# A patch-token, attention and expert layer: inner chunks in twos, their 64-row products in pairs on the two halves of the rows

## What is computed

```
logits = flat @ Wr                       # 8 experts, two chosen for each token
order = argsort(-score)[:, :capacity]    # capacity 3920 tokens for each expert
dispatch = flat[order]
gate = silu(einsum('ech,ehi->eci', dispatch, w1))     # h = 192, i = INNER = 768
up = einsum('ech,ehi->eci', dispatch, w3)
expert_out = einsum('eci,eih->ech', gate * up, w2) * weight_sel[..., None]
routed = zeros.at[order].add(expert_out)
shared = silu(flat @ s1) * (flat @ s3) @ s2
out = h + routed + shared
```

## Time and profile before

| what | value |
|---|---|
| median of three runs | 3695.66 us (3693.1 to 3698.46) |
| the profiled execution | 3705.55 us, span 3703.7 us |
| PE busy | 3398.9 us, 92% |
| PE weight loads busy | 2416.6 us, 65% |
| DVE busy | 2472.7 us, 67% |
| ACT busy | 1570.9 us, 42% |
| POOL busy | 1432.8 us, 39% |
| granted TensorE clock, mean | 0.87 |

### The profile page before, as it was taken

The page is one execution under the profiler, slowest core; times in us unless marked ns, Lnnn a source line. Parts: engine busy times, 40 slices in busy tenths (PEclk is TensorE's granted clock), DMA queues, the critical chain, the costliest instruction groups (busy, mean ns, idle before and its releaser), DMA issues. The chain is left out here.

```text
span 3703.7 us, 76882 instructions
## 1 busy us (share of the span) xinstructions
PE 3398.9 (92%) x26932; PEld 2416.6 (65%) x26932; DVE 2472.7 (67%) x4826; ACT 1570.9 (42%) x3198; POOL 1432.8 (39%) x1302
## 2 busy tenths in 40 slices
PE   5999999999999999998249999899999999999997
PEld 4777777777777777776226566666666666666665
DVE  5988898888888989897645555554454444445443
ACT  2444444444444445443014444344444444444443
POOL 0222232222222222232215553136556555555664
PEclk8787788877877888775569999999999999999999
DMA  3332333223323332222012222213232232323222
GB/s 95 71 69 61 75 82 69 68 70 80 69 62 75 82 69 73 65 53 56 35 50 63 66 72 71 83 31 66 38 61 42 59 63 39 60 38 61 41 40 31
DMA packets 330541, 227.05 MB, mean 61 GB/s; under 512 B 209103, under 2 KB 309551, under 8 KB 326159
## 3 DMA queue, kind: packets, MB, share of 16 engines
q1 hardware_dynamic: 259536, 163.94, 17.4%
q0 software_dynamic: 57472, 48.46, 8.8%
q10 hardware_dynamic: 13262, 10.65, 0.8%
HBM read 107.75 MB, written 67.85 MB: 47 GB/s over the span
## 5 line engine op out<-in xcount | busy, mean ns | idle before, releaser
L1272 DVE SCALAR_TENSOR_TENSOR ffn_hidden<-ffn_up,ffn_silu 128x490 f32<-128x490 f32 (+2 forms) x534 | 358.1, 672 | 802.3 <-ACT ffn_silu L1255 731.4
L699 POOL TENSOR_TENSOR weights<-weights,x_pair 128x400 f32<-128x400 f32 x384 | 397.2, 1034 | 918.1 <-DVE weights L563 733.7
L1255 ACT ACTIVATE ffn_silu<-ffn_gate 128x490 f32<-128x490 f32 (+2 forms) x534 | 310.9, 583 | 702.4 <-PE ffn_up L1223 635.7
L615 DVE RECIPROCAL recip<-x_product 128x200 f32<-128x200 f32 x384 | 534.4, 1392 | 0.0
L1240 PE MATMUL ffn_out<-ffn_w_hi,ffn_hidden_hi 128*126 128x192 f16 (+2 forms) x2124 | 522.5, 246 | 0.0
L1242 PE MATMUL ffn_out<-ffn_w_hi,ffn_hidden_lo 128*126 128x192 f16 (+2 forms) x2124 | 522.4, 246 | 0.0
L1241 PE MATMUL ffn_out<-ffn_w_lo,ffn_hidden_hi 128*126 128x192 f16 (+2 forms) x2124 | 522.3, 246 | 0.0
L1428 POOL DMA_INDIRECT out_rows<-done,kept x256 | 425.9, 1664 | 150.4 <-issue 98.1
L1418 POOL DMA_INDIRECT tokens<-dram_x,ids x256 | 279.6, 1092 | 397.5 <-issue 258.9
L750 PE MATMUL bank<-w_qkv,normed_t 96*128 96x192 f32 (+1 forms) x1024 | 399.8, 555 | 19.1 <-ACT normed_t L413 19.1
L1265 DVE TENSOR_TENSOR ffn_hidden_lo<-ffn_hidden,ffn_hidden_hi 128x490 f16<-128x490 f32 (+2 forms) x534 | 355.4, 666 | 8.4
(11 more groups left out here) (181 smaller groups left out, 7429.8 us busy)
## 6 DMA issues: line engine op xcount, KB each, us to landing
patches<-in_patches SPq DMA_DIRECT2D x32, 1176.0 KB, 5.1
ffn_raw<-in_w SPq DMA_DIRECT2D x18, 768.0 KB
dram_x_t<-x_t SPq DMA_DIRECT2D x32, 392.0 KB, 3.1
x_t<-dram_x_t SPq DMA_DIRECT2D x24, 512.0 KB, 5.2
base<-dram_h SPq DMA_DIRECT2D x24, 384.0 KB
out_rows<-sums ACTq DMA_DIRECT2D x24, 384.0 KB
v_held<-v SPq DMA_DIRECT2D x64, 102.0 KB, 2.3
dram_h<-h SPq DMA_DIRECT2D x32, 192.0 KB
```

The costliest lines, as they stand in the source:

```text
L615: nc.vector.reciprocal(recip[:, n % 2], x_product[:, n % 2]).then_inc(inverted, 1)
L699: nc.gpsimd.tensor_tensor(weights[:, n % 4], weights[:, n % 4], x_pair[:, n % 4, ::-1], ALU.mult)\
L1255: nc.scalar.activation(T.silu[:, m % 2, 0:n], T.gate[m % 2][:, 0:n], ACT.Silu, scale=1.0 / (TOKEN_SCALE * WEIGHT_SCALE)).then_inc(T.silued, 1)
L1272: nc.vector.scalar_tensor_tensor(T.hidden[:, m % 2, 0:n], T.up[m % 2][:, 0:n], HIDDEN_SCALE / (TOKEN_SCALE * WEIGHT_SCALE), T.silu[:, m % ...
```

## The change

The chunks of a unit go two at a time, in three blocks. In a block, the four products of each chunk and output that use all 128 rows come first, 16 in all. Then come the four with `w_lo` and the far high tokens: those for gate use rows 0 to 63, those for up rows 64 to 127, with `far_again`, a second copy of the far high tokens, in these rows. Each is a product of 64 rows, and the two of a chunk stand on the two halves. `gated` now rises twice for each chunk.

`tensor_out` is cut into thirds of eight (tile, chunk) groups, and one stands behind each block. `turn` stands behind the first block, ahead of the first third. The token tiles have two slots, and the splits of the next unit are made after silu 3 (ScalarE) and `hidden` 3 with `hidden_lo` 2 (VectorE), instead of after the last chunk. ScalarE makes one more activation there, of 64 rows. `w_lo` is made in all 128 rows, and the memsets go.

```diff
-            for w_lo in T.w_lo:
-                for lo in w_lo[0:2]:
-                    n += 1
-                    nc.gpsimd.memset(lo[D - 128:128, INNER:2 * INNER], 0.0).then_inc(enlarged, 1)
-                    pool.wait_ge(enlarged, n)
...
+def tokens_hi(nc, T, slot, near, far, n):
+
+    nc.scalar.activation(T.near_hi[slot][:, 0:n], near, ACT.Copy, scale=TOKEN_SCALE).then_inc(T.tokens_hi, 1)
+
+    nc.scalar.activation(T.far_again[slot][D - 128:128, 0:n], far[D - 128:128], ACT.Copy, scale=TOKEN_SCALE)
+    nc.scalar.activation(T.far[slot][:, 0:n], far, ACT.Copy, scale=TOKEN_SCALE).then_inc(T.tokens_hi, 1)
...
+def tensor_pair(nc, pe, T, g, slot, ws, n, pair):
+
+
+    if pair == 0:
+        pe.wait_ge(T.tokens_lo, 2 * g + 6)
+    near_hi, near_lo, far, far_again = (x[slot][:, 0:n] for x in (T.near_hi, T.near_lo, T.far, T.far_again))
+    top, low = slice(0, D - 128), slice(D - 128, 128)
+    for m in (2 * pair, 2 * pair + 1):
 
         pe.wait_ge(T.multiplied, MI * g + m + 1)
         near = slice(m * 128, (m + 1) * 128)
-        far = slice(INNER + m * 128, INNER + (m + 1) * 128)
+        beyond = slice(INNER + m * 128, INNER + (m + 1) * 128)
...
             nc.tensor.matmul(out, hi[:, near], near_hi, start=True, stop=False)
             nc.tensor.matmul(out, hi[:, near], near_lo, start=False, stop=False)
             nc.tensor.matmul(out, lo[:, near], near_hi, start=False, stop=False)
-            nc.tensor.matmul(out, hi[:, far], far_both, start=False, stop=False)
-            last = nc.tensor.matmul(out, lo[:, far], far_both, start=False, stop=True)
-        last.then_inc(T.gated, 1)
...
+            nc.tensor.matmul(out, hi[:, beyond], far, start=False, stop=False)
+    for m in (2 * pair, 2 * pair + 1):
+        beyond = slice(INNER + m * 128, INNER + (m + 1) * 128)
+        nc.tensor.matmul(T.gate[m % 2][:, 0:n], T.w_lo[ws][0][top, beyond], far[top], start=False, stop=True)\
+          .then_inc(T.gated, 1)
+        nc.tensor.matmul(T.up[m % 2][:, 0:n], T.w_lo[ws][1][low, beyond], far_again[low], start=False, stop=True)\
+          .then_inc(T.gated, 1)
...
+    share = len(tiles) * MI // 3
+    for k in range(third * share, (third + 1) * share):
+        t, m = divmod(k, MI)
...
     for m in range(MI):
-        act.wait_ge(T.gated, MI * g + m + 1)
+        act.wait_ge(T.gated, 2 * (MI * g + m + 1))
...
         if m:
             hi(m - 1)
+        if m == 3:
+            split()
     hi(MI - 1)
...
-                tensor_unit(nc, pe, T, g, ws, XU)
-                if not closing(e, i, 7):
-                    turn(v + 1, half + i % 2, 1 - i % 2)
...
+                for part in range(3):
+                    tensor_pair(nc, pe, T, g, 1 - i % 2, ws, XU, part)
+                    if part == 0 and not closing(e, i, 7):
+                        turn(v + 1, half + i % 2, 1 - i % 2)
...
+                        tensor_out(nc, pe, T, g - 1, i % 2, 1 - ws if i == 0 else ws, ROUTED, part)
```

More of the change, by code:

```diff
@@ L1145, in sb @@
         return ctx.enter_context(nc.sbuf_tensor(f"ffn_{name}", shape, dt))
[L1147 to L1149 removed]
+    T.near_hi, T.near_lo, T.far, T.far_again = (
+        [sb(f"tokens_{name}{s}", [128, ST], F16) for s in range(2)] for name in ("near_hi", "near_lo", "far", "far_again"))
     T.silu = sb("silu", [128, 2, ST])
@@ L1174, in lower_parts @@
 def lower_parts(T, ws):
-    near, far = (slice(0, 128), slice(0, INNER)), (slice(0, D - 128), slice(INNER, 2 * INNER))
-    whole = (slice(0, 128), slice(0, MI * D))
+    near, far, whole = slice(0, INNER), slice(INNER, 2 * INNER), slice(0, MI * D)
     for n, parts in enumerate(((near, far), (near, far), (whole,))):
         for part in parts:
-            yield T.raw[n][part], T.w_hi[ws][n][part], T.w_lo[ws][n][part], part is parts[-1]
+            yield T.raw[n][:, part], T.w_hi[ws][n][:, part], T.w_lo[ws][n][:, part], part is parts[-1]
 def weights_lo(nc, T, ws):
@@ L1231, in tensor_out @@
+def tensor_out(nc, pe, T, g, slot, ws, tiles, third):
+    if third == 0:
+        pe.wait_ge(T.lo_ready, MI * g + MI + 2)
     w_hi, w_lo = (w[ws][2][:].rearrange("p (m n) -> p m n", m=MI) for w in (T.w_hi, T.w_lo))
     per = len(tiles) // 2
[L1233 to L1243, removed]
@@ L1246, in scalar_unit @@
-def scalar_unit(nc, act, T, g, slot, n):
+    share = len(tiles) * MI // 3
+    for k in range(third * share, (third + 1) * share):
+        t, m = divmod(k, MI)
+        n, c = divmod(t, per)
+        if m == 0 and c == 0:
+            pe.wait_ge(T.out_used, 2 * g + n + 1)
+        at, rows = tiles[t]
+        out = T.out[n][0:rows, c * D:(c + 1) * D]
+        hi, lo = T.hidden_hi[slot][:, m, at:at + rows], T.hidden_lo[slot][:, m, at:at + rows]
+        nc.tensor.matmul(out, hi, w_hi[:, m, :], start=(m == 0), stop=False)
+        nc.tensor.matmul(out, hi, w_lo[:, m, :], start=False, stop=False)
+        last = nc.tensor.matmul(out, lo, w_hi[:, m, :], start=False, stop=(m == MI - 1))
+        if m == MI - 1 and c == per - 1:
+            last.then_inc(T.out_full, 1)
@@ L1247, in hi, with scalar_unit @@
+def scalar_unit(nc, act, T, g, slot, n, split):
     def hi(m):
@@ L1478, in unit @@
             def unit(g, half, slot, tiles):
[L1479 to L1483, removed]
+                for part in range(3):
+                    tensor_pair(nc, pe, T, g, slot, 0, columns_of(tiles), part)
+                    if part == 0 and tiles is SHORT:
+                        turn(0, 0, 0)
+                    if not (isinstance(g, int) and g == 0):
+                        tensor_out(nc, pe, T, g - 1, 1 - slot, 0, WHOLE, part)
             shared_units(pe, unit)
@@ L1537, in unit, with split_next @@
             def unit(g, half, slot, tiles):
[L1538 to L1544, removed]
+                def split_next():
+                    if tiles is SHORT:
+                        split(0, 1)
+                    elif isinstance(g, int) and g == SHARED - 2:
+                        split_shared(half + 1, 0, TAIL)
+                    else:
+                        split_shared(half + slot, 1 - slot, ST)
+                scalar_unit(nc, act, T, g, slot, columns_of(tiles), split_next)
                 if not (isinstance(g, int) and g == 0):
```

71 lines of the change are left out of this document (33 added, 38 removed).

## The result

The changed kernel took 3710.8 us (median of 20 runs), the kernel before 3696.7 us in the same comparison: a ratio of 1.0036, 95% interval 1.0021 to 1.0051. The change makes the kernel 0.36% slower. The forecast was 3699 us, with a range of 3664 to 3735 that holds the result; "slower", the likeliest of the three signs by a little, came true. The profiled execution took 3710.33 us, its span 3708.5 us.

The account below looks back on a forecast made before the run. TensorE was taken to set the pace. Routed units -7, weights +21, shared units -14, seam +5 and tail -1 sum to +4 us on a profiled 3705.55 us; with the median 10 us lower, 3699 us, range 3664 to 3735.

Parts of the forecast that it names:

- slower: Sign of the forecast: the kernel's time rises by more than 0.2%; chance 0.39, against faster 0.34 and same 0.27.
- Products: TensorE's routed unit: halves save 1.24 us, mode switches cost 0.6, so 19.60 becomes 18.96 us.
- Case E: Rival: halves of the rows don't run together, routed unit 20.2 us, kernel 3774 us; chance 0.06.
- Order: Between blocks: a third of the output (1.97 us) covers the 1.6 us of clearing `gate` and `up`; no cost.
- The wait that takes the place: Routed units: earlier transposes wait for gathered rows, 19.48 us a unit, so 62 units gain 7 us, not 40.
- the cycle: Routed stage: transposes, rest of unit, `put`, scatter, landing, ids, gather, transposes; 38.96 us for two units.
- Case C: Rival: VectorE's bunched work collides with gathers and scatters, path 19.6 us, unit 19.98, kernel 3730 us; chance 0.22.
- Weights for the next expert: Seven expert starts: `hidden` 3.4 us late, scatter 3.8 late, 4.0 us together against 1.0 now; 21 us lost.
- Shared units: Shared stage: halves save 1.30 us less 0.6 of switching; 0.6 us a unit taken, 14 us gained.
- The seam: From shared to routed units: more work stands behind the first wait for rows; about 5 us lost.
- wrong altogether: What would refute the forecast: a clock that falls in the 4 us gaps of TensorE; no size given.
- Case A: The forecast itself: the rows cycle eats the gain, 3699 us, own range 3685 to 3713; chance 0.45.

Follow-up runs that it names:

- e1: The changed kernel with the remainder products as 128-row products again (halves undone), its order kept: 3731.7 us, ratio 1.0118.
- e5: The changed kernel with halves in the old order (blocks back to back, then transposes, then all output): 3891.5 us, ratio 1.057.
- e2: The changed kernel with the transposes of the next unit's rows behind block 2 instead of block 1: 3675.3 us, ratio 0.9961.
- b9: The kernel before with weights one matrix at a time (units 1, 3, 5), an expert's units written out, ids asked for early: 3695.5 us, ratio 1.0013.
- b10: b9 with also the first expert's weights made one at a time, in shared units 19, 21 and 22: 3685.6 us, ratio 0.9995.
- e6: The changed kernel with the first ids asked for ahead of the last shared unit's loads: 3695 us, ratio 1.0023.
- e4: The changed kernel with ScalarE's output evictions ahead of the bunch of three weight matrices behind unit 1: 3721 us, ratio 1.0063.
- e9: The changed kernel with transposes behind block 2 and b10's weights, written-out units and early ids: 3633.0 us, ratio 0.985.

## Why the prediction was right, point by point

- **Products.** Right. The doubled increments of `gated` and the extra activation, costed at nothing, cost nothing: e1 has both, and its units are the old 19.60 and 18.89 us. The switch was taken at 0.2 us a block and measures 0.25, so the unit is 19.11 us and not 18.96. The Trainium skill (TensorEngine Tiling (Array Packing), Key Properties) says that a change of mode drains TensorE; the trace agrees, with 0.1 us on either side of the pairs. Case E, halves that don't run together, is out.
- **Order.** Right: no wait ahead of blocks 2 and 3, and e5 shows 1.2 us at each without the thirds (1.6 was estimated).
- **The wait that takes the place.** Right, and the core of the forecast. 36.6 us at the transposes, released by the gather; e2 takes one block and a third out of the cycle, and they vanish. The path was 19.33 and 1.68 us in the one cycle shown, which is at an expert's start, against 18.6 and 2.0 (the 2.0 and its bound of 1.3 had no row). Of the 61 steps from unit to unit, the 39 under 20.3 us average 19.45, and 19.48 was forecast. Case C's collisions did not come: the scatters last 1.60 us on average (212 of them, 2560 to 3642 us), 1.66 in the earlier trace rows.
- **Weights for the next expert.** The step was right, the arithmetic not. It said that the 3.4 us before `hidden` and the 3.8 us of a late scatter "run beside each other", 4.0 in all. They stand one behind the other: 2.6 us, and 1.7 to 1.9 at six of the next transposes. The two units around the start, 2580.92 to 2623.81, take 42.9 us where 38.2 is their own: 4.7 a time, where the old order loses 1.15 (20.75 for 19.60).
- **Shared units.** 24.9 us gained, 14 forecast. The unit's own work fell by 0.66 us (18.89 to 18.23, forecast 0.6), 24 times 15.8, and e1's units of 18.89 show that this is the halves'. Of the other 9.1 us, 2.2 are the halved clock in unit 1 of the old order, which b9 and b10 have too. Some 6.6 are stalls of the profiled execution in units 6 to 16 (the 5.8 us of the earlier trace rows), which the forecast named and left out of its sum. The new order is not shown to have removed these: b9 has the old program in these units and none of the stalls (456.28 us against 462.86). Against b9 the gain is 18.3 us.
- **The seam.** 7.8 us lost, 5 forecast. The forecast took the 8.1 us of waiting for `hidden` there for a part of the routed stage; the new order hid them in its wait of 17.85 us for rows, as e6 shows.
- **What was missing.** The halved clock behind waits: it is most of the 17.6 us left over in the changed kernel, against 6.4 before. In units 2 to 62 the clock was at 0.50 in seven stretches, 27.3 us together, against 10.2 us in two before. The forecast named it as what would be "wrong altogether" and gave it no price. The routed units lost 28.8 us, the forecast has 14 for them (-7 + 21); the 11.2 us more of left-over time are most of the difference.

The errors in the shared units and in the routed ones have opposite signs, and that the forecast's +4 us lies so near the +4.8 of the two spans is luck: the medians say +14.1. The mechanism doesn't hang on this luck, as e2 shows. Case A's own range, 3685 to 3713, holds the result, near its upper end.

## What to carry to other kernels

When an order is stretched so that engines meet more evenly, walk every cycle that passes through the moved step, also those that did not bind before: here the transposes were needed two blocks earlier and their rows came no earlier. The change was not wrong but unfinished; putting the transposes one block later turned +0.4% into -0.4%, and taking its other new waits away made -1.5%, while the same repairs did next to nothing for the old order. An old stop, at the loop's jump, was worth another 0.4%. Look too for what hides in a wait before removing it (the first expert's weights), and for the load that waits on the buffer of a step which is put off.

## What was not expected of the hardware

- A wait of TensorE can cost half as much again in clock. After waits of 5.3 us (the changed kernel), 3.8 to 4.6 (e4), and 1.65 and 2.64 close together (e2, five times of seven), the granted clock fell to its 1.2 GHz level, and 1.8 to 3.5 us were lost each time. Two windows of the changed kernel, behind the wait of 5.28 us and behind one of 2.64 before `hidden`, which ended at 3249.91:

```profile
2867.00:2872.00 5.00, 5.00 (x13) 1.91 (x14) 0.00 (x0) 0.00 (x0) 4.14 (x3) 0.50 0.55 59
3251.20:3254.60 3.40, 3.40 (x10) 1.27 (x9) 0.00 (x0) 0.00 (x0) 2.93 (x2) 0.50 0.57 57
```

  Behind the other six single waits of 2.6 us before `hidden` it stayed at 2.4 GHz. In e6, with the same routed units, the clock fell behind four of the seven, and in e1 behind five. It also fell behind waits of 2.5, 1.92 and 1.85 us before the transposes, and not behind others as long. So waits of 1.8 to 2.6 us sometimes cost clock and sometimes not; what decides it stays open.
- The jump back of the loop over experts stops TensorE twice, for 5.3 and 4.0 us in the changed kernel, and for 2.5 to 6.3 us each in the other versions. In e9 the two stops are 4.2 and 3.8 us. Written out straight, seven experts of eight units have no such stop, and the clock's loss behind it is gone too: 13.5 us less in units 2 to 62 (1184.4 to 1170.9), 17 in the medians. The rival's argument, that code without the jump has to be fetched all the same, showed in no row.
